# Attention, then a pooled non-local block, on one core: one row sum group a chunk instead of two, and values in quarters of a tile

## What is computed

```python
qkv = einsum('oc,bchw->bohw', w_qkv, x)
q, k, v = split(qkv, 3, axis=1)            # each (2, 8, 32, 4096)
scores = einsum('bhdi,bhdj->bhij', q, k) / sqrt(32)
attn = softmax(scores, axis=-1)
out = einsum('bhij,bhdj->bhdi', attn, v)
x = einsum('oc,bchw->bohw', w_proj, out) + x
```

## Time and profile before

| | |
|---|---|
| median of 3 runs | 2491.8 us (2490.13 to 2494.98) |
| the profiled execution | 2491.46 us |
| its span in the profile | 2489.8 us |
| mean granted TensorE clock | 0.994 |
| busy: TensorE matmuls | 2431.2 us, 98% |
| busy: ScalarE | 2227.4 us, 89% |
| busy: VectorE | 2137.3 us, 86% |
| DMA queue that GpSimd feeds | 54.0% of 16 engines |

### The profile page before, as it was taken

How to read it: one execution, slowest core, us unless ns; L and a number is a source line. 1 busy time by engine, 2 the same in 40 slices (tenths; PEclk the granted TensorE clock), 3 DMA queues, 4 the chain that set the end, 5 groups by cost and what they waited for, 6 DMA issues and landing times.

```text
span 2489.8 us, 74134 instructions
## 1 busy us (share of the span) xinstructions
PE 2431.2 (98%) x33040; PEld 1082.5 (43%) x33044; DVE 2137.3 (86%) x1338; ACT 2227.4 (89%) x1842; POOL 455.8 (18%) x652
## 2 busy tenths in 40 slices
PE   8999999999999999999999999999999999999997
PEld 4444444444444444344444444444444444443443
DVE  6999999969999999895579999999799999998854
ACT  7999999979999999566589999999899999995763
POOL 0222222202222222110002222222022222220200
PEclk9999999999999999999999999999999999999999
DMA  7877777767777877601277777777677777774011
GB/s 241 164 157 158 161 160 160 153 181 151 161 159 156 163 157 152 164 1 73 85 195 160 162 156 159 158 158 157 176 159 161 159 157 158 161 153 131 1 64 39
DMA packets 150257, 359.98 MB, mean 145 GB/s; under 512 B 23088, under 2 KB 65392, under 8 KB 149680
## 3 DMA queue, kind: packets, MB, share of 16 engines
q0 software_dynamic: 73728, 268.47, 54.0%
q1 hardware_dynamic: 76208, 86.78, 11.3%
HBM read 52.63 MB, written 33.85 MB: 35 GB/s over the span
## 4 chain that ended last, share of the span: by engine, by line
PE 73%; ACT 17%; issue 4%; DVE 2%; SPq 2%; DMA 1%; ACTq 0%; POOL 0%
PE scores L528 27%; PE psOL L541 27%; ACT arena L610 16%; PE psOL L965 7%; PE scores L349 3%; PE psOL L889 1%; PE scores L360 1%; PE scores L952 1%; PE scores L953 1%; DVE arena L659 1%; PE scores L942 1%; SPq L1253 1%; DMA att_inv<-Ls 1%; PE scores L943 1%; PE psOL L512 1%
## 5 line engine op out<-in xcount | busy, mean ns | idle before, releaser
L610 ACT ACTIVATE arena<-scores 128x1536 f32<-128x1536 f32 x1368 | 1849.9, 1463 | 8.6 <-PE scores L528 5.9
L659 DVE TENSOR_TENSOR arena<-arena 128x2048 f32<-128x2048 f32 x732 | 1674.7, 2291 | 126.7 <-ACT arena L610 74.9
L528 PE MATMUL scores<-arena 96*32 96x512 f16 x16384 | 1128.1, 380 | 13.6 <-ACT arena L610 12.1
L541 PE MATMUL psOL<-arena 128*32 128x256 f32 (+1 forms) x13120 | 1107.2, 432 | 0.0
L528 PEld LDWEIGHTS scores<-arena 96*32 96x32 f16 x16384 | 399.8, 95 | 700.3 <-ACT arena L610 389.6
L688 POOL DMA_DIRECT2D arena<-arena x448 | 387.9, 893 | 1131.2 <-ACT arena L610 844.0
L541 PEld LDWEIGHTS psOL<-arena 128*32 128x32 f32 x13120 | 391.2, 110 | 343.0 <-issue 8.7
L965 PE MATMUL psOL<-arena 128*128 128x512 f16 x768 | 170.3, 379 | 0.0
L685 POOL DMA_DIRECT2D arena<-arena x64 | 35.2, 554 | 567.6 <-ACT arena L610 567.3
L1230 DVE SCALAR_TENSOR_TENSOR arena<-arena 128x1536 f16<-128x1536 f32 (+1 forms) x48 | 75.9, 1581 | 66.8 <-ACT arena L1082 64.9
L1075 ACT ACTIVATE arena<-scores 128x1536 f32<-128x1536 f32 (+1 forms) x48 | 62.4, 1300 | 72.7 <-PE scores L953 72.7
(11 more groups left out here) (118 smaller groups left out, 1168.8 us busy)
## 6 DMA issues: line engine op xcount, KB each, us to landing
arena<-arena POOLq DMA_DIRECT2D x512, 512.0 KB, 5.4
arena<-qk_parts SPq DMA_DIRECT2D x192, 128.0 KB, 3.8
qk_parts<-arena SPq DMA_DIRECT2D x32, 512.0 KB, 3.6
X<-in_x SPq DMA_DIRECT2D x16, 512.0 KB, 4.5
att_out<-arena SPq DMA_DIRECT2D x32, 256.0 KB, 3.9
arena<-att_out SPq DMA_DIRECT2D x16, 512.0 KB, 10.7
out<-arena SPq DMA_DIRECT2D x32, 256.0 KB, 2.0
arena<-att_inv SPq DMA_DIRECT2D x16, 256.0 KB
```

The source lines that it names most:

```text
L528: last = nc.tensor.matmul(bank[k % 2][m * D:(m + 1) * D, i * CH:(i + 1) * CH], KS[0:3 * D, h, j * 128 + m * D:j * 128 + (m + 1) * D], QS2[ ...
L541: last = nc.tensor.matmul(both(c)[h * D:(h + 1) * D, lo:hi], V[:, j, h * D:(h + 1) * D], P[:, r + h, lo:hi], start=(j == 0), stop=(j == JT ...
L610: nc.scalar.activation(P[:, u % RING:u % RING + size, :], bank[k % 2][:, 0:size * CH].rearrange("p (u n) -> p u n", n=CH), ACT.Exp, scale= ...
L659: nc.vector.tensor_tensor(new, old, P[:, r:r + G, :], ALU.add).then_inc(s_add, 1)
```

## The change

- The two sums over partitions of a chunk (one of `acc`, one of `accD`) become one, 16 steps after the chunk's last exponential, for seven of the eight chunks. For that GpSimd issues two more adding DMAs at the end of these chunks, which add `accD` onto `acc`; they wait for VectorE's last addition of the chunk and for the last DMA into `accD`. The last chunk keeps its two groups, now in one function, `sums_of_last`.
- The values are handed out in quarters of a tile (128 columns) in place of halves. A step's share is cut at tile borders, so a piece has 1 to 4 quarters and each piece is one set of matmuls. `rate` is 3.09 quarters a step.
- The flags that start and stop accumulation stand on the first and last piece of a chunk's PSUM bank.
- Counts of semaphores follow: `s_sum` counts one a chunk, `s_merge` is new.

```diff
-SUMS_A, SUMS_D, BEHIND = 8, 20, 2
-SUM_STEPS = sorted(exps_through(c, JT - 1) + d for c in range(NC - 1) for d in (SUMS_A, SUMS_D))
+SUMS, BEHIND = 16, 4
+SUM_STEPS = [exps_through(c, JT - 1) + SUMS for c in range(NC - 1)]
...
-def halves_by_step():
+def quarters_by_step():

-    rate = (2 * JT + 4) * GROUP / (G * JT)
-    first = exps_through(0, JT - 1) + SUMS_A
-    start = first - (first * GROUP / 2 - BEHIND) / rate
+    rate = 4 * (JT + 1) * GROUP / (G * JT)
+    first = exps_through(0, JT - 1) + SUMS
+    start = first - (first * GROUP - BEHIND) / rate
     done, at = [], 0
     for k in range(GROUPS):
-        ready = 2 * (min((k + 1) * GROUP, UNITS) // G)
-        share = int(rate * (k + 1 - start)) - 2 * sum(1 for n in SUM_STEPS if n <= k)
-        to = ready if k == GROUPS - 1 else min(ready, share)
-        to -= to % (2 * JT) in (1, 2 * JT - 1)
-        at = max(at, to)
+        ready = 4 * (min((k + 1) * GROUP, UNITS) // G)
+        share = int(rate * (k + 1 - start)) - 4 * sum(1 for n in SUM_STEPS if n <= k)
+        at = ready if k == GROUPS - 1 else max(at, min(ready, share))
         done.append(at)
     return done
...
             s_dma = [sem(root, f"s_dma{k}_{g}") for k in range(2)]
+            s_merge = [sem(root, f"s_merge{k}_{g}") for k in range(2)]
...
-            def sums_of_acc(pe, c):
-                if c < NC - 1:
-                    pe.wait_ge(s_o_free, c + 1)
...
+            def sums_of_merged(pe, c):
+                pe.wait_ge(s_o_free, c + 1)
+                for k in range(2):
+                    pe.wait_ge(s_merge[k], 16 * (c + 1))
                 for h in range(G):
-                    last = nc.tensor.matmul(sums_in(c)[h * D:(h + 1) * D, :], ones[:], acc[c % 2][:, h, :],
-                                            start=(c < NC - 1), stop=False)
+                    last = nc.tensor.matmul(both(c)[h * D:(h + 1) * D, :], ones[:], acc[c % 2][:, h, :],
+                                            start=True, stop=True)
                 last.then_inc(s_sum, 1)
...
-                                                P[:, r + h, lo:hi], start=(j == 0), stop=(j == JT - 1))
+                                                P[:, r + h, lo:hi], start=(j == 0 and lo == 0),
+                                                stop=(j == JT - 1 and hi == CH))
...
                     for c in range(NC - 1):
-                        if k == exps_through(c, JT - 1) + SUMS_A:
-                            sums_of_acc(pe, c)
-                        if k == exps_through(c, JT - 1) + SUMS_D:
-                            sums_of_dma(pe, c)
-                    at, end = HALVES[k - 1] if k else 0, HALVES[k]
+                        if k == exps_through(c, JT - 1) + SUMS:
+                            sums_of_merged(pe, c)
+                    at, end = QUARTERS[k - 1] if k else 0, QUARTERS[k]
                     while at < end:
-                        n, odd = divmod(at, 2)
-                        if odd or at + 1 == end:
-                            values(n, odd * CH // 2, (odd + 1) * CH // 2)
-                            at += 1
-                        else:
-                            values(n, 0, CH)
-                            at += 2
+                        n, lo = divmod(at, 4)
+                        hi = min(4, lo + end - at)
+                        values(n, lo * CH // 4, hi * CH // 4)
+                        at += hi - lo
...
             def sums_out(dve, c):
-                dve.wait_ge(s_sum, (c + 1) * 2)
+                dve.wait_ge(s_sum, c + 1)
...
                                 pool.wait_ge(s_dma[k], 16 * (c * len(SUM_D) + i))
                                 nc.gpsimd.dma_start(dst, src, accum_op=ALU.add).then_inc(s_dma[k], 16)
+                    if c < NC - 1:
+                        pool.wait_ge(s_add, adds_by(c))
+                        for k in range(2):
+                            hs = slice(2 * k, 2 * k + 2)
+                            pool.wait_ge(s_dma[k], 16 * len(SUM_D) * (c + 1))
+                            nc.gpsimd.dma_start(acc[c % 2][:, hs, :].rearrange("p h n -> p (h n)"),
+                                                accD[c % 2][:, hs, :].rearrange("p h n -> p (h n)"),
+                                                accum_op=ALU.add).then_inc(s_merge[k], 16)
```

More of the change, by code:

```diff
@@ L61, in adds_through @@
     return max(1, sum(1 for t in SUM_V if t <= j) - 1)
-SUMS_A, SUMS_D, BEHIND = 8, 20, 2
-SUM_STEPS = sorted(exps_through(c, JT - 1) + d for c in range(NC - 1) for d in (SUMS_A, SUMS_D))
-def halves_by_step():
-    rate = (2 * JT + 4) * GROUP / (G * JT)
-    first = exps_through(0, JT - 1) + SUMS_A
-    start = first - (first * GROUP / 2 - BEHIND) / rate
+SUMS, BEHIND = 16, 4
[4 more added lines that the diff above has]
+    start = first - (first * GROUP - BEHIND) / rate
     done, at = [], 0
     for k in range(GROUPS):
-        ready = 2 * (min((k + 1) * GROUP, UNITS) // G)
-        share = int(rate * (k + 1 - start)) - 2 * sum(1 for n in SUM_STEPS if n <= k)
-        to = ready if k == GROUPS - 1 else min(ready, share)
-        to -= to % (2 * JT) in (1, 2 * JT - 1)
-        at = max(at, to)
+        ready = 4 * (min((k + 1) * GROUP, UNITS) // G)
+        share = int(rate * (k + 1 - start)) - 4 * sum(1 for n in SUM_STEPS if n <= k)
+        at = ready if k == GROUPS - 1 else max(at, min(ready, share))
         done.append(at)
     return done
-HALVES = halves_by_step()
+QUARTERS = quarters_by_step()
 BY_DMA = [3, 4, 5, 6]
@@ L485, in sums_in, with sums_of_last @@
             def sums_in(c):
-                return (psO, psL)[c % 2] if c < NC - 1 else psO
+                return both(c) if c < NC - 1 else psO
             def adds_by(c):
                 return (c + 1) * ADDS - (c == NC - 1)
-            def sums_of_acc(pe, c):
-                if c < NC - 1:
-                    pe.wait_ge(s_o_free, c + 1)
-                else:
[L497 to L502, removed]
+            def sums_of_merged(pe, c):
+                pe.wait_ge(s_o_free, c + 1)
+                for k in range(2):
+                    pe.wait_ge(s_merge[k], 16 * (c + 1))
                 for h in range(G):
-                    last = nc.tensor.matmul(sums_in(c)[h * D:(h + 1) * D, :], ones[:], acc[c % 2][:, h, :],
-                                            start=(c < NC - 1), stop=False)
+                    last = nc.tensor.matmul(both(c)[h * D:(h + 1) * D, :], ones[:], acc[c % 2][:, h, :],
+                                            start=True, stop=True)
                 last.then_inc(s_sum, 1)
-            def sums_of_dma(pe, c):
+            def sums_of_last(pe):
+                pe.wait_ge(s_l_free, NC - 1)
+                r = (NC * JT - 1) * G % RING
+                for h in range(G):
+                    nc.tensor.matmul(psO[h * D:(h + 1) * D, :], ones[:], P[:, r + h, :], start=True, stop=False)
+                pe.wait_ge(s_add, adds_by(NC - 1))
+                for h in range(G):
+                    nc.tensor.matmul(psO[h * D:(h + 1) * D, :], ones[:], acc[(NC - 1) % 2][:, h, :],
+                                     start=False, stop=False)
                 for k in range(2):
-                    pe.wait_ge(s_dma[k], 16 * len(SUM_D) * (c + 1))
+                    pe.wait_ge(s_dma[k], 16 * len(SUM_D) * NC)
                 for h in range(G):
-                    last = nc.tensor.matmul(sums_in(c)[h * D:(h + 1) * D, :], ones[:], accD[c % 2][:, h, :],
+                    last = nc.tensor.matmul(psO[h * D:(h + 1) * D, :], ones[:], accD[(NC - 1) % 2][:, h, :],
                                             start=False, stop=True)
@@ L566, in tensor @@
                     for c in range(NC - 1):
-                        if k == exps_through(c, JT - 1) + SUMS_A:
-                            sums_of_acc(pe, c)
-                        if k == exps_through(c, JT - 1) + SUMS_D:
-                            sums_of_dma(pe, c)
-                    at, end = HALVES[k - 1] if k else 0, HALVES[k]
-                    while at < end:
-                        n, odd = divmod(at, 2)
-                        if odd or at + 1 == end:
-                            values(n, odd * CH // 2, (odd + 1) * CH // 2)
-                            at += 1
-                        else:
-                            values(n, 0, CH)
-                            at += 2
+                        if k == exps_through(c, JT - 1) + SUMS:
+                            sums_of_merged(pe, c)
+                    at, end = QUARTERS[k - 1] if k else 0, QUARTERS[k]
+                    while at < end:
+                        n, lo = divmod(at, 4)
+                        hi = min(4, lo + end - at)
+                        values(n, lo * CH // 4, hi * CH // 4)
+                        at += hi - lo
             def tensor_end(pe):
-                sums_of_acc(pe, NC - 1)
-                sums_of_dma(pe, NC - 1)
+                sums_of_last(pe)
             def slot_free(act, m):
@@ L681, in gpsimd @@
```

(13 more changed lines are left out.)

## The result

The changed kernel takes 2478.0 us (median of 6 runs, 2474.5 to 2481.0), the kernel before 2491.0 us in the runs beside it; the ratio is 0.9944 with a 95% interval of 0.9933 to 0.9954. That is 13 us where 31 were forecast. The time lies in the range, at its upper end, but the size was wrong. Rival C, "half the gain", gave 2475 to 2480; that is what came, though VectorE, which it named, was not the reason, and neither was the price of short pieces.

The account below looks back on a forecast made before the run. TensorE and ScalarE were taken as equally loaded, 454.5 and 454.6 us an attention, losing time by uneven hand-over; even steps would take 31 us off 2491.8, giving 2461 us, range 2452 to 2480.

Parts of the forecast that it names:

- Rival C: In the attentions, 0.06 us extra a quarter piece or VectorE's thin cover halves the gain: 2475 to 2480 us, chance 0.10.
- Two engines with the same work, losing by uneven hand-over: In each attention, TensorE has 454.5 us of work, ScalarE 454.6; 9.3 us is lost, 8.3 of it to unevenness.
- of the measured 8.3 us some 7.8 go: Waiting from uneven TensorE steps in each attention nearly vanishes with quarters: 31 us over four attentions.
- ScalarE's pace of 1.333 us: Exponentials in an attention start 1.333 us apart, so 341 of them set a floor of 454.6 us.
- The tally by hand: TensorE's lateness carried from step to step: 6.6 to 8 us of waiting an attention before, 0.3 to 0.5 with quarters.
- Merging DMAs hidden: At chunk borders, two added DMAs issue in GpSimd's idle stretch and land 7 us before the row sum.
- the copies behind them may land up to 5.2 us later: The next chunk's copies queue behind the merging DMAs; ScalarE doesn't wait, as their tile is overwritten 16 us after exponentiation.
- Rival D: Added DMAs come late at chunk borders, ScalarE waits for slots of tile 6 or 9: 28 us, 2489, chance 0.05.
- Row sums bring slack and no time: Seven groups of 0.86 us leave TensorE in each attention, 6.0 us; ScalarE's floor doesn't move.
- Short pieces at 0.004 us: On TensorE, each one-quarter piece of values costs 0.004 us extra: 0.7 us for 166, inside its slack of 6.1.
- VectorE's thin cover: VectorE's work is 56.3 us in a chunk of 56.9, enough but thin; its waits fall below 10 us an attention.
- A: The forecast itself: ScalarE runs at its own pace, 2461 us, own range 2452 to 2470, chance 0.72.

Follow-up runs that it names:

- e1: The kernel before with only the values changed to quarters, two row sum groups a chunk and no merging DMAs: 2474.9 us, ratio 0.9934.
- e2: The changed kernel with the values in halves again, one row sum group and the merging DMAs kept: 2493.2 us, ratio 1.0008.
- e3: The changed kernel without the merging DMAs, the DMAs' tiles left out of the row sums of chunks 0 to 6: 2471.7 us, ratio 0.9926.
- e5: e3 with the value pieces of tiles 1 to 30 also cut to half of their columns: 2470.1 us, ratio 0.9916.
- e4: The changed kernel with the DMAs' tiles moved away from the chunk's start, everything computed: 2489.0 us, ratio 0.9981.
- e6: e3 with the DMAs' tiles moved to 4, 8, 11, 14, 17, 20, 23, 27: 2483.3 us, ratio 0.9960.

## Why the prediction was wrong, point by point

- **Two engines with the same work, losing by uneven hand-over:** right in kind, wrong in size. e1 changes only the evenness and gets 17 us; e2 keeps the halves and gets none. But the term "of the measured 8.3 us some 7.8 go", 31 us in all, was mis-sized: 4.7 us an attention were there to be had, and e3 has 0.2 of them left, some 18 us over four.
- **ScalarE's pace of 1.333 us:** this is the step that failed first, and the reason for that size. It was read from the starts of six exponentials, and the starts run ahead. Looked at one by one, the first of them starts at 860.37 and lasts 1.46 us and the sixth starts at 867.04 and lasts 1.50: their ends are (868.54 - 861.83) / 5 = 1.342 us apart. The pace is 1.343, and the floor of an attention 458.0 us, not 454.6. That is 3.4 us an attention, 13.6 of the 18.9 us by which the attentions missed (31 forecast, 12.1 got from first to last start). The 9.3 us above the floor were 5.9, of which 1.2 on average at the starts, and TensorE, with 454.5 us, never had as much work as ScalarE. The tally by hand counted against the same 1.333, and so could come near the 9.3. With 1.343 it comes out: it gave 3.1 us an attention for e2, and e2's trace has 3.2 beside the starts and the one wait for a DMA.
- **Merging DMAs hidden:** the second failed step, 7.7 us. Both waits were put right: GpSimd issues in its idle stretch, and the sum comes long after the merge. What was missing is the order on the queue: "the copies behind them may land up to 5.2 us later" was written down and taken as harmless, since a slot has 16 us. That size was right: the copies land 5.5 us later (3.8 to 9.3). But the next tile's DMAs wait for the copies, and the one after for those, so the delay is handed on to tile 9. Rival D named tile 6 or 9, at 28 us, and had 0.05.
- These two are 21.3 us; the attentions' starts gave back 2.3: 4.8 us over the pace before, 2.5 after. That is luck as far as the runs show. The start of an attention loses time where TensorE's granted clock is low in its first 15 us, and which attention that is changes from kernel to kernel: the second and third before (0.78, 0.88), the fourth after (0.89), the second and fourth in e1 (0.89, 0.77), none in e3.
- **Row sums bring slack and no time:** right for quarters, where e1 keeps 14 row sums an attention and e3 has 7, and both, beside their starts, stand within 1 us of the floor over the four attentions, and right for e2's time as a whole. In e2's attentions it did bring 6.1 us.
- **Short pieces at 0.004 us:** right, nothing to be seen.
- **VectorE's thin cover:** right that it doesn't bind; its waits for exponentials are 60.4 / 4 = 15.1 us an attention, not below 10, since the chunks shrank less.
- **The measured time inside the range:** luck. It is the number of rival C, half the gain, whose reasons (0.06 us a short piece, or VectorE) the trace doesn't show. And the chances of A, C and half of D add up to 0.845, not 0.86.

## What to carry to other kernels

Read the pace of a saturated engine from the ends of its instructions, or from start to start over a stretch long enough to hold the correction; a length that grows from one instruction to the next says that the starts run ahead. Where DMAs wait for one another in a chain, put added ones behind the transfer that starts the chain, not ahead of it: a delay there is handed on to every later link. And when two engines are equally loaded, cut the work into even steps before taking work away from either.

## What was not expected of the hardware

An exponential of 128x1536 lasts 1.463 us in the record on average before, 1.583 after and 1.700 in e5, with the ends 1.343 to 1.344 us apart (median) in all three. The length says how long ScalarE has had work waiting, not how much it works. This lead is also a reserve: a start that TensorE holds back to 1.45 us behind the one before costs nothing while the exponential before is still running. In e4, the granted clock fell to 1.2 GHz in TensorE's wait of 6.5 us at the end of an attention and stayed there for what came next (1.93 us for eight matmuls of 1.04); the stretch was 7.3 us longer in all than in the changed kernel, a little more than the wait itself. The same stands behind the wait of 6.3 us in e6 (1.94 us).
